# A two-layer transformer with expert layers: twelve row buffers for the expert tiles, and expert weights split in smaller steps

## The reference

```python
shared = _silu_and_mul(x @ shared_gate_up_w.T) @ shared_down_w.T
shared = shared * jax.nn.sigmoid(x @ shared_gate_w.T)
probs = softmax(x @ gate_w.T)
routing_weights, selected_experts = jax.lax.top_k(probs, TOP_K)   # 2 of 8
for e in range(E):
    w_e = jnp.where(selected_experts == e, routing_weights, 0.0).sum(-1)
    combined += w_e[:, None] * (_silu_and_mul(x @ w13[e].T) @ w2[e].T)
out = shared + combined
```

## Time and profile before

| | us |
|---|---|
| median of three runs | 1602.81 (1602.20 to 1607.62) |
| the profiled execution | 1605.1 |
| its span, first to last instruction | 1603.0 |

### The profile page before, as it was taken

How to read it: one execution, slowest core, us unless ns; L and a number is a source line. 1 busy time by engine, 2 the same in 40 slices (tenths; PEclk the granted TensorE clock), 3 DMA queues, 4 the chain that set the end, 5 groups by cost and what they waited for, 6 DMA issues and landing times. The chain is left out here.

```text
span 1603.0 us, 29414 instructions
## 1 busy us (share of the span) xinstructions
PE 1475.6 (92%) x10844; PEld 1127.3 (70%) x10844; DVE 990.4 (62%) x2156; ACT 756.5 (47%) x1872; POOL 534.0 (33%) x448
## 2 busy tenths in 40 slices
PE   6999999998899989999999989998998898999897
PEld 4778877777788677777777758885555686633587
DVE  5766676666564666666565556557664745476754
ACT  5565656655335334343433434433443353577243
POOL 2836537262137163334133012532000371100074
PEclk9999999999999999999999999989999999999999
DMA  4122221221543532202012018234000633000424
GB/s 153 56 75 90 83 82 59 77 71 64 202 181 103 179 96 86 94 13 96 29 61 78 1 33 340 77 103 173 2 2 5 217 103 115 1 1 1 182 93 138
DMA packets 53900, 144.88 MB, mean 90 GB/s; under 512 B 8721, under 2 KB 23441, under 8 KB 53649
## 3 DMA queue, kind: packets, MB, share of 16 engines
q1 hardware_dynamic: 36496, 84.99, 15.2%
q0 software_dynamic: 17280, 58.21, 10.6%
HBM read 104.90 MB, written 38.27 MB: 89 GB/s over the span
## 5 line engine op out<-in xcount | busy, mean ns | idle before, releaser
L145 POOL TENSOR_SCALAR ln_var<-ln_moments 128x4 f32<-128x4 f32 x16 | 4.0, 251 | 415.9 <-DVE ln_moments L130 261.5
L397 POOL DMA_INDIRECT s_xg<-normed_rows,s_from_row x92 | 93.1, 1012 | 107.0 <-DVE s_from_row L802 80.2
L404 POOL DMA_INDIRECT expert_rows<-s_y,s_to_row x92 | 91.1, 990 | 72.6 <-ACT s_y L688 51.6
L1300 ACT ACTIVATE s_scratch<-s_bank,s_neg_max 128x128 f32<-128x128 f32 (+3 forms) x128 | 67.3, 528 | 89.6 <-DVE s_neg_max L1390 89.4
L1390 DVE TENSOR_REDUCE s_neg_max<-s_bank 128x1 f32<-128x128 f32 (+3 forms) x128 | 59.5, 486 | 54.1 <-PE s_bank L1190 53.9
L1188 PE MATMUL s_bank<-s_k,s_q 128*128 128x128 f32 (+3 forms) x256 | 88.6, 441 | 1.5 <-DVE s_v L1385 0.8
L2699 POOL TENSOR_TENSOR s_w_hi<-s_w_raw,zero 128x1024 fp32r<-128x1024 f32 x25 | 55.7, 2229 | 102.7 <-PE s_memory L81 79.7
L894 DVE TENSOR_TENSOR s_h_e<-s_bank,s_silu_e 128x176 f32<-128x176 f32 x92 | 31.4, 341 | 93.3 <-ACT s_silu_e L676 91.1
L2384 ACT ACTIVATE s_exps<-s_bank,s_rms 128x512 f32<-128x512 f32 x128 | 76.7, 696 | 21.4 <-PE s_bank L2264 21.4
L1400 DVE TENSOR_SCALAR s_scratch<-s_scratch,s_row_sum 128x128 f32<-128x128 f32 (+3 forms) x128 | 80.5, 629 | 4.5
L79 PE MATMUL s_bank<-xn_t_hi,s_w_hi 128*128 128x512 f32 x192 | 80.1, 417 | 0.7 <-DVE s_w_lo L2403 0.4
(11 more groups left out here) (421 smaller groups left out, 4864.6 us busy)
## 6 DMA issues: line engine op xcount, KB each, us to landing
s_expert_w_lo<-experts_lo SPq DMA_DIRECT2D x32, 608.0 KB, 13.5
s_expert_w_hi<-experts_hi SPq DMA_DIRECT2D x16, 608.0 KB, 12.3
s_w_raw<-in_wa_o SPq DMA_DIRECT2D x16, 512.0 KB, 3.6
s_yg<-expert_rows SPq DMA_DIRECT2D x32, 256.0 KB, 4.7
s_raw<-in_shared SPq DMA_DIRECT2D x16, 384.0 KB, 5.5
s_e_lo<-in_experts POOLq DMA_DIRECT2D x16, 304.0 KB, 3.1
experts_hi<-s_e_hi POOLq DMA_DIRECT2D x16, 304.0 KB, 2.5
experts_lo<-s_e_lo POOLq DMA_DIRECT2D x16, 304.0 KB, 2.9
```

The lines of the kernel that those rows point to most:

```text
L397: pool.indirect_dma_start(out=xg[:, i % XG_RING, :], out_offset=None, in_=x_rows[:, :], in_offset=bass.IndirectOffsetOnAxis(ap=from_row[:, ...
L404: pool.indirect_dma_start(out=y_rows[:, :], out_offset=bass.IndirectOffsetOnAxis(ap=to_row[:, i:i + 1].bitcast(U32), axis=0), in_=y[:, i % ...
L1300: act.activation(probs[:, h % 2, r, 0:(r + 1) * P], score_bank(h, r), ACT.Exp, bias=neg_max[:, 4 * h + r:4 * h + r + 1], accum_out=row_sum ...
```

## The change

- `XG_RING` goes from 8 to 12. `xg` keeps eight slots; slots 8 to 11 are the first four token blocks of `norm.xn`, which has been stored to DRAM by then (`rows_in`). So twelve gathers stand ahead of scatter 0.
- In s2 a piece has 608 columns instead of 1216, and there are 16 of them. Four stand ahead of the second group as two did; in each later group two stand behind the split of k and two behind that of v, where two large ones stood behind v.
- In both stages hi and lo of a piece are made in two steps of 304 columns each, so four shorter instructions instead of two.
- The start stage's semaphores come from `Semaphores`, under which they are cleared and reused like the others.

```diff
-XG_RING, Y_RING = 8, 8
+XG_RING, Y_RING = 12, 8
...
-        xg, y = sb("xg", [P, XG_RING, D]), sb("y", [P, Y_RING, D])
+        xg, y = sb("xg", [P, Y_RING, D]), sb("y", [P, Y_RING, D])
...
+        def rows_in(i):
+            at = i % XG_RING
+            return xg[:, at, :] if at < Y_RING else norm.xn[:, at - Y_RING, :]
...
                 pool.indirect_dma_start(
-                    out=xg[:, i % XG_RING, :], out_offset=None, in_=x_rows[:, :],
+                    out=rows_in(i), out_offset=None, in_=x_rows[:, :],
...
                     last = pe.transpose(xt_bank[i % 2][:, c * P:(c + 1) * P],
-                                        xg[:, i % XG_RING, c * P:(c + 1) * P], res.ident[:])
+                                        rows_in(i)[:, c * P:(c + 1) * P], res.ident[:])
...
         if by_run:
-            expert_split = ExpertSplit(nc, ctx, sem, name, res, t["experts1"], t["experts1_parts"], EXP_COLS)
+            expert_split = ExpertSplit(nc, ctx, sem, name, res, t["experts1"], t["experts1_parts"], E_PART)
...
             if by_run:
-                for n in range(2):
-                    expert_split.piece(pool, n, n, 0, n == 0)
+                for n in range(4):
+                    expert_split.piece(pool, n, n // 2, n % 2 * E_PART, n == 0)
             for i in range(1, GROUPS):
-                split(i, (0, 1))
-                if by_run:
-                    for n in range(2):
-                        expert_split.piece(pool, 2 * i + n, 2 * i + n, 0)
-                split(i, (2,))
+                for p in range(3):
+                    split(i, (p,))
+                    if by_run and p < 2:
+                        for n in range(4 * i + 2 * p, 4 * i + 2 * p + 2):
+                            expert_split.piece(pool, n, n // 2, n % 2 * E_PART)
                 move_q(i)
             if by_run:
-                expert_split.end(pool, N_EXP)
+                expert_split.end(pool, 2 * N_EXP)
...
-        pool.tensor_tensor(self.hi[:], f32(self.lo[:]), self.res.zero[:].broadcast_to([P, self.columns]), ALU.add).then_inc(self.hi_done, 1)
-        pool.wait_ge(self.hi_done, n + 1)
-        pool.tensor_tensor(self.lo[:], f32(self.lo[:]), f32(self.hi[:]), ALU.subtract).then_inc(self.lo_done, 1)
+        half = self.columns // 2
+        for h in range(2):
+            some = slice(h * half, (h + 1) * half)
+            pool.tensor_tensor(self.hi[:, some], f32(self.lo[:, some]), self.res.zero[:].broadcast_to([P, half]), ALU.add).then_inc(self.hi_done, 1)
+        for h in range(2):
+            some = slice(h * half, (h + 1) * half)
+            pool.wait_ge(self.hi_done, 2 * n + h + 1)
+            pool.tensor_tensor(self.lo[:, some], f32(self.lo[:, some]), f32(self.hi[:, some]), ALU.subtract).then_inc(self.lo_done, 1)
...
-        loaded = ctx.enter_context(nc.semaphore("start_loaded"))
-        made = ctx.enter_context(nc.semaphore("constants_made"))
+        sem = ctx.enter_context(Semaphores(nc, "start"))
+        loaded, made = sem("loaded"), sem("constants_made")
```

More of the change, by code:

```diff
@@ L3225, in piece @@
         pool.wait_ge(self.loaded, 16 * n + 16)
-        pool.tensor_tensor(self.hi[:], f32(self.lo[:]), self.res.zero[:].broadcast_to([P, self.columns]), ALU.add).then_inc(self.hi_done, 1)
-        pool.wait_ge(self.hi_done, n + 1)
-        pool.tensor_tensor(self.lo[:], f32(self.lo[:]), f32(self.hi[:]), ALU.subtract).then_inc(self.lo_done, 1)
+        half = self.columns // 2
[6 more added lines that the diff above has]
+            pool.tensor_tensor(self.lo[:, some], f32(self.lo[:, some]), f32(self.hi[:, some]), ALU.subtract).then_inc(self.lo_done, 1)
         pool.dma_start(of(self.parts[0]), f32(self.hi[:])).then_inc(self.stored, 16)
-        pool.wait_ge(self.lo_done, n + 1)
+        pool.wait_ge(self.lo_done, 2 * n + 2)
         pool.dma_start(of(self.parts[1]), f32(self.lo[:])).then_inc(self.stored, 16)
```

## The result

The changed kernel takes 1586.47 us in the median of four runs, the kernel before 1603.18: the ratio is 0.9887, with a 95% interval of 0.9858 to 0.9915, so 1.1% faster. The forecast was 1584.5 in a range of 1577.0 to 1593.5. Two of its three terms came out as worked out. The middle one, the pieces, did not, and most of the experiments are about it.

The account below looks back on a forecast made before the run. TensorE, busy 92%, bounds the kernel; gains come from its idle 127 us. 13.8 (ring) + 5.5 (pieces) - 1.2 (clears) = 18.1 us off 1605.1 gives 1587.0; runs' median 2.3 lower: 1584.7, rounded 1584.5, range 1577 to 1593.5.

Parts of the forecast that it names:

- the pieces: Smaller pieces and shorter steps in s2 free VectorE's normalisations, so TensorE's waits go: 5.5 us, bounds 0 and 6.1.
- The ring: Twelve gathers ahead in the expert loops: 4.0 us in s1, 5.0 in s3, 2.5 in s5, 2.3 in s7; 13.8 together.
- Rivals A: Rival A: the tails of s5 and s7 don't hang on the scatters; 3.3 us more gain, 1581, chance 0.12.
- C: Rival: in s5 and s7 the four gathers stretch to 1.91 us, losing 1.3 and 1.5 us; 1592, chance 0.08.
- the 648.13 row: In s2, a normalisation running its usual 0.29 us across a GpSimd step change, read as VectorE getting in between steps.
- rival D: The shared port pair never passes to VectorE between GpSimd's steps in s0 and s2; 19.7 us slower, 1622, chance 0.04.
- the v split: In s2 the split of the v weights moves at most 8.7 us later; GpSimd is mostly idle, so charged 0.
- Rival B: Shorter steps don't relieve VectorE, since twice as many pieces land in s2's q fills; the 5.5 us go, 1590, chance 0.18.
- The clears: More semaphore clears at the entries of s2, s4, s6 and the end: four at 0.3, 1.2 us lost; one at s0, 0.

Follow-up runs that it names:

- e8: The changed kernel with ten slots in place of twelve; 1586.97 us, ratio 0.9903 to the kernel before.
- e2: The changed kernel with eight slots and the old start semaphores, so pieces and steps alone; 1602.68 us, ratio 1.0001 to the kernel before.
- e1: The kernel before with only the twelve slots; its rival said the FFN gain came partly from the clock. 1587.44 us, ratio 0.9898.
- e4: The changed kernel with s2's pieces at old places and old size (8 of 1216 columns), steps of 608; 1584.68 us, ratio 0.9883.
- e6: The changed kernel with s2's 8 pieces of 1216 columns at old places, hi and lo each in eight steps of 152; 1582.79 us, ratio 0.9877.
- e10: The kernel before with hi and lo of each s2 piece in eight steps of 152 columns (s0: four), old places, eight slots; 1593.84 us, ratio 0.9959.
- e5: The changed kernel with steps not halved (608 columns at once, s0 and s2), pieces at new places; 1585.07 us, ratio 0.9890.
- e9: The changed kernel run and traced again without an edit; 1583.51 us, ratio 0.9886 to the kernel before.
- e3: The changed kernel with the k, v and o weight splits in s2 in four steps of 256 columns too; 1582.09 us, ratio 0.9850.
- e12: The changed kernel with s2's pieces at old places, steps of 152, and attention weight splits of s0 and s2 in steps of 256; 1579.56 us, ratio 0.9859.

## Why the prediction was right, and where it was not

**The ring: right, step by step.** Means over three profiles with eight slots and ten with twelve: s1 127.8 and 123.1, s3 126.6 and 121.7, s5 101.4 and 98.5, s7 102.4 and 100.1. That is 4.7, 4.9, 2.9 and 2.3 us, 14.8 in all; the sum had 4.0, 5.0, 2.5 and 2.3, 13.8. The reasoning on s5 and s7, that four more gathers ahead push scatter 0 back by 3.7 us and that the gain is then cut to what GpSimd's row of 46 transfers allows, is what e8 and the rows of after show. Rivals A and C both fall: scatter 22 of s5 is issued at 1311.32, 2.3 us after its y is written, and the four gathers are not stretched. ScalarE's write of that y in the timeline:

```profile
1308.59 0.39 ACT L692 ACTIVATE s_y<-s_bank 128x256 f32<-128x256 f32 x1 [0.57 <-PE s_bank L81]
```

For the last y of s1 the prediction took 524.06, which is the issue of its scatter; ScalarE had written that y by 523.49 (523.10 and 0.39 long). Nothing hangs on the difference.

Of s3 the reading was half luck. Its 26.10 us from tile 12 to 22, an outlier among 25.1 and 25.2, contain a stretch of lower clock (columns of the windows: busy us and count of PE, PEld, DVE, ACT, POOL, then the granted clock, DMA share and GB/s):

```profile
1030.00:1040.00 10.00, 8.08 (x56) 6.92 (x54) 4.02 (x12) 4.77 (x14) 7.61 (x8) 1.00 0.34 106
1041.00:1045.00 4.00, 4.00 (x22) 3.89 (x20) 1.37 (x4) 2.01 (x6) 2.97 (x4) 0.58 0.30 101
```

It begins right behind this wait of TensorE, the longest for s_xg in that trace (start, us, instruction, idle before):

```profile
1040.59 0.44 PE L525 MATMUL s_bank<-ident,s_xg 128*128 128x128 f32 x2 [1.85 <-DMA s_xg<-normed_rows,s_from_row]
```

e2 has the same in s1, behind a wait of 2.02 us:

```profile
508.42 0.44 PE L529 MATMUL s_bank<-ident,s_xg 128*128 128x128 f32 x2 [2.02 <-DMA s_xg<-normed_rows,s_from_row]
```

```profile
510.00:514.00 4.00, 4.00 (x20) 3.90 (x19) 1.25 (x4) 1.67 (x5) 2.95 (x3) 0.57 0.31 98
```

Two of the six loops of s1 and s3 with eight slots have such a drop, worth near 1.7 us (0.42 of 4 us); of the 22 with ten or twelve slots none has. The other four loops with eight slots give a gain of 3.9 us in s1 and 4.0 in s3, so the 5.0 that the sum had for s3 was 4.0 of pace and a stretch of lower clock, as the rival of e1 said. The ring therefore gives more than the sum of the waits it removes, now and then. In s5 some of the 2.9 us comes from the stretched gather that is missing in six profiles (see e8); the four profiles with two gain 2.3.

**The pieces: the term was mis-sized, 5.5 us for some 2.** Over the profiles of old code (369.8 and 367.9) and of new (366.5, 368.3, 364.4, 367.8) the inside of s2 went from 368.9 to 366.7 (some 3 us in place of 2 if the stretches of lower clock in e2 and e9 are taken off), and e2 sees no gain at all. Two steps failed, and the second took the gain.

The first is "what VectorE can lose at a stroke falls from 2.8 to 0.85 us" with "freed, it ends 2 us earlier ... so the 1.63 us go whole". That VectorE gets in between GpSimd's steps was read rightly off the 648.13 row, and rival D falls with it. But the loss was then counted for one operation. VectorE has a row of normalisations there, each can meet the next step, and the loss is up to the number of operations times the step: e4 halved the steps and kept the loss. The loss vanishes when the steps are so short that three or four of them don't matter (e6, e10). In the changed kernel itself the pieces' own steps make no wait over 0.48 us, but e5 shows that in groups three and four the new places do that without shorter steps.

The second is the v split, "so I charge 0 for it". The reason, that GpSimd is idle most of the time, answers whether the split is late for TensorE; it isn't. It doesn't answer what the split's own two steps, 1.91 and 2.35 us and not touched by the change, hold up at their new moment. In the second group they fell on the normalisations ahead of a q fill: 1.48 us in after, 3.69 in e2, 3.48 in e9, 2.76 in e5, 1.33 in e8. The k split, which four pieces in place of two now push back and which the prediction does not name, did the same to s_v: 1.70 us in after. e3 removed the waits by shortening the steps of the splits alone. The v split also moved further than the 8.7 us that the prediction allowed. Its first step before, and the load of the second piece ahead of it after:

```profile
637.48 1.89 POOL L1094 TENSOR_TENSOR s_w_hi<-s_w_raw,zero 128x1024 fp32r<-128x1024 f32 x1 [17.57 <-DMA s_w_raw<-in_wb_v]
```

```profile
637.32 0.54 POOL L3228 DMA_DIRECT2D s_e_lo<-in_experts  x1 [8.00 <-DMA experts_lo<-s_e_lo]
```

From the start of the inner stretch it stood at 56.35 us (637.48 less 581.13) and stands at 67.95 (644.55 less 576.60), 11.6 us later: a piece waits for the stores of the one ahead of it, here 8.00 us, and the 8.7 had no such wait in it. Rival B named the right outcome, the gain gone, by the wrong culprit.

The Trainium skill ("SBUF — State Buffer", "Terms") says that the holder of the port pair keeps it for the full instruction and the other blocks. The runs agree: in the rows of after, e4 and e9 every held normalisation ends 0.1 to 0.25 us behind a step's end. It leaves open who is next. In the rows of e4 it is VectorE, behind each step, and over the fourteen traces some nine in ten of the held normalisations end with the step that they met. The others wait longer. In e12 one lasts 1.66 us, until the third of GpSimd's last three steps of some 0.5 us is over:

```profile
656.93 2.87 POOL L3244 TENSOR_TENSOR s_e_lo<-s_e_lo,s_e_hi 128x152 fp32r<-128x152 f32 x6
...
658.42 1.66 DVE L1408 TENSOR_SCALAR s_scratch<-s_scratch,s_row_sum 128x512 f32<-128x512 f32 x1
```

What decides it no run here shows. The Trainium skill also says ("SBUF — State Buffer", "SBUF: two separate sides") that whoever starts first gets the pair. That can't be read off here: the normalisation of e9 at 640.46 starts 0.47 us ahead of the recorded start of the GpSimd step that holds it, and the profile's spans of GpSimd are rough. The same section of the Trainium skill counts only some VectorE operations as users of the pair. This agrees: the evacuations that read PSUM (L1380) take 0.56 to 0.64 us, beside GpSimd steps and without them.

**The clears: right.** 0.27 to 0.28 us each at three entries and at the end, against 0.3.

So the total was met, 18.1 against 17.4 in the profiled executions, although the pieces gave about 3 us less than their term. That it came so near is luck in part. By the means the ring gave 1 us more, which makes 14.8 + 2.1 - 1.1 = 15.8; the 1.6 us that are left are within what executions differ by, and the interval of the ratio (13.6 to 22.8 us) holds either.

## What to carry to other kernels

When work on GpSimd shares the port with VectorE, count the loss as up to the number of VectorE operations that can meet it times the length of one GpSimd instruction; in e4 halving the instructions did nothing while VectorE had twice as many operations to be held, and in e6 cutting them to the length of those operations ended it. When such work is moved, look at every long instruction that it pushes to a new moment, not only at the one that was moved. A ring ahead of a loop is deep enough once the slower side's lag is covered to the last tile; more slots only shift the order of the same issues.

## What was not expected

TensorE's clock fell to its lower level at the end of, or within 1.7 us behind, single waits of 1.85, 2.02, 3.48 and 3.69 us in the middle of busy stretches: granted 0.58 (before, 1041 to 1045), 0.57 (e2, 510 to 514), 0.57 (e9, 646 to 650) and 0.57 (e2, 653 to 657). It did not behind others as long: the 1.9 us in e10, the 2.04 in e1 and the 2.76 in e5, where it stayed at 1.00. If the waits are the cause, which no experiment tested, one can cost almost twice its own length; which of them does, no run here settles.

Steps of 152 columns cost GpSimd 0.45 us (hi) and 0.54 us (lo) each in e6 (groups by line and shape: count, busy us, mean ns, idle before):

```profile
L3237 POOL TENSOR_TENSOR s_e_lo<-s_e_lo,s_e_hi 128x152 fp32r<-128x152 f32 x128 | 65.0, 540 | 0.0
L3233 POOL TENSOR_TENSOR s_e_hi<-s_e_lo,zero 128x152 fp32r<-128x152 f32 x128 | 54.2, 453 | 71.1 <-DMA s_e_lo<-in_experts 71.1
```

Steps of 304 columns cost 0.69 and 0.83, so the fixed part of an instruction is about 0.2 to 0.25 us, an estimate from these means. Eight steps in place of one made the same work some 1.5 times as long (3.22 against 2.21 us in the rows of e6), and all of it was hidden.
